# Weight sums of a seven-product scheme: high and low parts stored apart, low parts in two buffers, high parts' stores issued by ScalarE

## The chip, the cores and the metric

The kernel runs on one core of one Trainium2 chip. The metric is the device time in microseconds (us) of one launch; lower is better. The time before is 3198.1 us, the median of three runs (3197.61 to 3199.45).

## What is computed

Two branches read the same input x of 8192 tokens by 512 channels and are added to it: a state-space layer followed by a two-layer MLP with GELU (512 to 2048 to 512), and a gated feed-forward layer with block-wise FP4 rounding. The change lies in the preparation of the first MLP matrix w1.

```
xn = layernorm(x)
x  = x + attn_ref(xn, ...) + ffn_ref(xn, w_gate, w_up, w_down)
# inside attn_ref
x = x + ssm_scan(rmsnorm(x, scale1), A, B, C, D)
h = rmsnorm(x, scale2)
h = gelu(h @ w1 + b1) @ w2 + b2          # the MLP
return x + h
```

All of it is in float32. The kernel splits each factor of a matrix product into a high part (fp32r, a rounded copy) and a low part (the difference), and adds three products, high by high, high by low and low by high.

## The kernel before

The program first does the FP4 branch and the state-space layer (up to about 1750 us of the trace). The MLP follows in two manners. The first eight token tiles of 128 tokens, two blocks of four, are done plainly in a loop over steps n = 2 to 33: `mlp1(n)` is 12 matmuls into one bank (one slice of 128 hidden units), `gelu(n)` on ScalarE turns it into `gf`, `gelu_parts(n)` on VectorE makes its high and low parts, and `mlp2(n - 2)` is 12 more matmuls. Behind ScalarE's `gelu(n)` stands the wait for `mlp1(n)`, and `mlp1(n + 2)` waits for `gelu(n)`. In steps 2 to 13 ScalarE (`w_high`, line 1923) and VectorE (`w_low`, line 1527) also split the weight slice n + 2 that `mlp1(n + 2)` needs.

The other 56 tiles are done in seven pairs of blocks with a seven-product scheme (lines 1193 and 1215), which needs sums of quarters of w1. These sums are made beside the plain steps, in 16 rounds k. The helper `combine_steps` puts round k at step 3 + 4k//3, so three rounds fall on each four steps (3, 4, 5, 7, 8, 9, 11, ... 23). A round is, by engine:

- SyncE (SP), step of k less 1 or earlier: `combine_load` (line 751) loads a piece of w1 into `wt[:, k % 2]`, once `combine_low(k - 2)` is done.
- ScalarE (ACT): `combine_scale(k)` (line 1973), two instructions in `wt`.
- GpSimd (POOL): `combine_sums(k)` (lines 2201 to 2206), four sums of 128x128.
- ACT, one step later: `combine_high(k)` (line 1981) writes `wh`, of 128x1024. It waits for the sums and, through the count of `d_wa`, until both stores of round k - 1 have landed.
- POOL, the same step: `combine_low(k)` (line 2210), `wl = wt - wh`. It has no wait for a store of its own; that of `combine_high` covers it.
- SP, two steps after the round's own: `combine_store(k)` (line 759) stores `wh` and `wl`, 512 KB each, into `r_A` in device memory.

From step 18 on `ring_load` (line 768) reads `r_A` back into the ring of 14 buffers that the products read.

Every engine runs its instructions in program order, and the order within a step matters. On ACT a step is: `w_high(n + 2)`, `gelu(n)`, `combine_scale`, `combine_high`, then the work on a token tile (`tile_high`, line 1947, or `tile_square`, line 1929). On SP it is: `combine_store`, `combine_load`, then the loads and stores of a token tile. In steps 3 to 11 this is `quadrants` (lines 830 and 833: a store to `r_H`, a wait until it has landed, four loads back). In steps 15 to 25 it is, for each of the tiles 8 to 15 in turn, `store_sum` (716, `r_Q`), `store_normed` (720, `r_N`), `z_load` of the next tile (712, `zl`, which waits until the `r_Q` store has landed), and `pre_load` two tiles ahead (695 and 699, `xl` and two of `yl`). Two such tiles fall on three steps. POOL's `tile_z` (2189, 2192) adds into `zl`, and `store_sum` waits for it. At steps 24, 25, 29 and 31 SP also loads turned tiles (`quarters`, line 739), which VectorE's `conv_turn` (line 1600) transposes and ACT's `conv_high` (lines 2001 to 2010) splits; the first `conv_high` waits for all stores of the sums.

Of the kernel before, what the change touches and what calls it, by code (L numbers as in the profile page):

```python
# [5 lines left out]
ALU = mybir.AluOpType  # L6
ACT = mybir.ActivationFunctionType
F32 = mybir.dt.float32
F32R = mybir.dt.float32r
# [3 lines left out]
P = 128  # L13
TOK = 8192
NT = TOK // P
# [30 lines left out]
STEPS = ((A11, B11, 4), (S2, T2, 5), (S3, T3, 6), (A12, B21, 4), (S1, T1, 7), (A22, T4, 6), (S4, B22, 7))  # L46
OPENS = (0, 1, 2, 4)
WSC0, WSUM0, WAH0, WAL0, HT0 = 4 * NST, 4 * NST, 3, 4, 11
RING_0, OQ_0, ZQ_0, WT_0, Q_0, WA_0, QO_0 = 32, 16, 8 * NT, 16, 16, 16, 16
QUADS = ((0, 1), (2, 3), (4, 0), (1, 2))  # L50
TURNED = ((4, 0), (1, 2), (3, 4), (0, 1))
SECOND = [(0, f) for f in range(14)] + [(1, 0), (1, 1), (0, 14), (0, 15)] + [(1, f) for f in range(2, 16)]
# [139 lines left out]
def combine_steps(n):  # L192

    return [k for k in range(16) if 3 + 4 * k // 3 == n]
# [14 lines left out]
def build(nc, x, A, B, C, Dv, sc1, sc2, w1, b1, w2, b2, wg, wu, wd, cst, out):  # L209
# [12 lines left out]
    r_A = nc.dram_tensor("r_A", [8, 8, P, 512], F32, kind="Internal").ap()  # L222
    r_s = nc.dram_tensor("r_s", [D * NST], F32, kind="Internal").ap()

    with ExitStack() as ctx:
        def sbt(c, name, shape, dt=F32):
            return c.enter_context(nc.sbuf_tensor(name, shape, dt))

        def sem(name):
            return ctx.enter_context(nc.semaphore(name))  # L230

        def sems(name, n):
            return [sem(f"{name}{i}") for i in range(n)]
# [65 lines left out]
        mctx = ExitStack()  # L299
# [28 lines left out]
        with ExitStack() as later:  # L328
            u2 = sbt(later, "u2", [P, D])
            u3 = sbt(later, "u3", [P, D])  # L330
            G2x = sbt(later, "G2x", [P, 2, D], F32R)
        zx1 = sbt(mctx, "zx1", [P, 4, D])
        st = sbt(mctx, "st", [P, D])
        s1 = sbt(mctx, "s1", [P, D])
        with ExitStack() as later:
# [3 lines left out]
            HC = sbt(later, "HC", [P, 5, 2, 2, D], F32R)  # L339
        wt = sbt(mctx, "wt", [P, 2, 8, P])  # L340
        wh = sbt(mctx, "wh", [P, 8, P], F32R)
        wl = sbt(mctx, "wl", [P, 8, P], F32R)
        assert nc.sbuf_base == base_ssm
        hT0 = [sbt(mctx, f"hT0{h}", [P, KD, D], F32R) for h in range(2)]
        zx0 = sbt(mctx, "zx0", [P, 4, D])
# [40 lines left out]
        s_wsc, s_wsum, s_wah, s_wal, s_ht = s_kC, s_kK, s_ka, s_kR, s_kd  # L386
# [4 lines left out]
        d_cs, d_kin, d_xin, d_px = sem("d_cs"), sems("d_kin", 6), sems("d_xin", 4), sems("d_px", 4)  # L391
        d_rs, d_a128, d_rW, d_rK = sem("d_rs"), sem("d_a128"), sems("d_rW", 2), sem("d_rK")
# [5 lines left out]
        d_xl, d_yl, d_zl, d_oo = sems("d_xl", 2), sems("d_yl", 2), sem("d_zl"), sems("d_oo", 8)  # L398
        d_ho, d_hi = sems("d_ho", 2), sems("d_hi", 2)
        d_ring, d_oq, d_zq, d_wt, d_q, d_wa, d_qo = d_wl[0:14], d_oo[0:4], d_px, d_kin[0:2], d_kin[2:4], d_kin[4], d_kin[5]  # L400

        def slot(t):
            return 0 if t < 4 else t % 2
# [82 lines left out]
        def combined(m, h):  # L486

            if m < 5:
                return HC[:, m, h]
            return WH[:, 4 * (m - 5) + 2 * h:4 * (m - 5) + 2 * h + 2, 0:D]  # L490

        def ring(q):
            return Wp[q % 14][1][:, 0]
# [37 lines left out]
        def sync_program(e):  # L531
# [118 lines left out]
            def z_out(t):  # L650
                e.wait_ge(s_z, t + 1)
                e.dma_start(r_Z[t], xin[:, 2 + t % 2]).then_inc(d_zo[t % 2], 16)
# [90 lines left out]
            def combine_load(k):  # L743
                if k >= 16:
                    return
                u, kt = k // 2, k % 2
                if k == 0:
                    e.wait_ge(s_dn, NW)
                if k >= 2:
                    e.wait_ge(s_wal, WAL0 + k - 1)  # L750
                e.dma_start(wt[:, k % 2, 0:4].rearrange("p (a f) c -> p a (f c)", a=2),
                            bass.AP(w1.tensor, kt * P * 2048 + 256 * u, [[2048, P], [2 * P * 2048, 2], [1, 256]])
                            ).then_inc(d_wt[k % 2], 16)

            def combine_store(k):
                u, kt = k // 2, k % 2
                for h in range(2):
                    e.wait_ge((s_wah, s_wal)[h], (WAH0, WAL0)[h] + k + 1)
                    e.dma_start(bass.AP(r_A.tensor, u * 8 * P * 512 + 256 * h + P * kt, [[512, P], [P * 512, 8], [1, P]]),
                                (wh, wl)[h][:].bitcast(F32)).then_inc(d_wa, 16)  # L760

            def ring_load(q):
                if q >= 56 * PAIRS:
                    return
                if q < 14:
                    e.wait_ge(s_w1, 17 + q)
                    e.wait_ge(d_wa, WA_0 + 32 * 4)
                e.dma_start(ring(q).bitcast(F32), r_A[q // 7 % 8, STEPS[q % 7][0]]).then_inc(d_ring[q % 14], 16)  # L768

            def residual_in(c, i):  # L770
# [165 lines left out]
            for n in range(2, 16 * NB1 + 2):  # L936
                if n == 2:
                    z_out(NT - 2)
                    z_out(NT - 1)
                for k in combine_steps(n - 2):  # L940
                    combine_store(k)
                for k in combine_steps(n - 1):
                    combine_load(k + 2)
                if (n - 2) % 16 == 15:
                    for j in range(4):
                        t = 4 * ((n - 2) // 16) + j
                        e.wait_ge(s_o, t + 1)
                        e.dma_start(ot[t], zx[(n - 2) // 16 % 2][:, j]).then_inc(d_oo[t % 8], 16)
                for t, part in mlp_steps(n):
                    prepare(t, part)  # L950
                for o, part in early_steps(n):
                    if part == 1:
                        store_sum(o)
                        store_normed(o)
                        z_load(o + 1)
                        if o < OLD + 6:
                            pre_load(o + 2)
                        else:
                            quarters(0, o - OLD - 6)
                if 18 <= n < 32:  # L960
                    ring_load(n - 18)
                if n in (29, 31):
                    quarters(0, (n - 25) // 2)
# [298 lines left out]
        def vector_program(e):  # L1262
# [328 lines left out]
            def conv_turn(c, i):  # L1591

                e.wait_ge(d_q[i % 2], Q_0 + 128 * (2 * c + i // 2 + 1))
                if i == 0 and c:
                    e.wait_ge(s_hch, 20 * c)
                    e.wait_ge(s_hcp, 8 * c)
                for j in range(2):
                    if i or j:
                        e.wait_ge(s_ht, HT0 + 8 * c + 2 * i + j)
                    e.transpose(place5[TURNED[i][j]][:], place5[QUADS[i][j]][:]).then_inc(s_ht, 1)  # L1600
# [167 lines left out]
        def scalar_program(e):  # L1768
# [206 lines left out]
            def combine_high(k):  # L1975
                e.wait_ge(s_wsum, WSUM0 + 4 * (k + 1))
                if k:
                    e.wait_ge(d_wa, WA_0 + 32 * k)
                else:
                    e.wait_ge(s_dn, NW)  # L1980
                e.activation(wh[:], wt[:, k % 2], ACT.Copy).then_inc(s_wah, 1)

            def conv_high(c, i, x):
                HA, HB = [place5[TURNED[i][j]] for j in range(2)]
                ba, bb = sum_banks(c, i)
                at = slice(i * P, (i + 1) * P)
                if c == 0 and i == 0 and x == 0:
                    e.wait_ge(s_w1, 24)
                    e.wait_ge(d_wa, WA_0 + 32 * 16)
                    for j in range(4):  # L1990
                        e.wait_ge(d_oo[j], 16)
                elif c and i == 0 and x == 0:
                    e.wait_ge(s_p, 56 * c)
                if x < 2:
                    e.wait_ge(s_ht, HT0 + 8 * c + 2 * i + 2)
                elif x == 2:
                    e.wait_ge(s_ts, 16 * c + 4 * i + 3)
                else:
                    e.wait_ge(s_ts, 16 * c + 4 * i + 4)
                if x == 0:  # L2000
                    e.activation(HC[:, B11:B21 + 1, 0, :, at], HA[:].rearrange("p (m k t) -> p m k t", m=2, k=2),
                                 ACT.Copy).then_inc(s_hch, 1)
                elif x == 1:
                    e.activation(combined(B22, 0)[:, :, at], HB[:, 256:512].rearrange("p (k t) -> p k t", k=2),
                                 ACT.Copy).then_inc(s_hch, 1)
                elif x == 2:
                    e.activation(HC[:, T1:T3 + 1, 0, :, at], ba[:].rearrange("p (m k t) -> p m k t", m=2, k=2),
                                 ACT.Copy).then_inc(s_hch, 1)
                else:
                    e.activation(combined((T2, T4)[x - 3], 0)[:, :, at],  # L2010
                                 bb[:, 256 * (x - 3):256 * (x - 2)].rearrange("p (k t) -> p k t", k=2),
                                 ACT.Copy).then_inc(s_hch, 1)
# [72 lines left out]
        def gpsimd_program(e):  # L2085
# [121 lines left out]

            def combine_low(k):
                e.wait_ge(s_wah, WAH0 + k + 1)
                e.tensor_tensor(wl[:], wt[:, k % 2], wh[:].bitcast(F32), ALU.subtract).then_inc(s_wal, 1)  # L2210

            def conv_low(c, i):
                HA, HB = [place5[TURNED[i][j]] for j in range(2)]
# [120 lines left out]
```

## Time and profile before

| | us |
|---|---|
| median of three runs | 3198.1 |
| the profiled execution, its own time | 3199.24 |
| span of its trace | 3197.4 |
| TensorE matmul busy | 3016.1 |
| VectorE busy | 2179.4 |
| GpSimd busy | 1599.9 |
| ScalarE busy | 1156.7 |

PE is TensorE's matmul side, DVE is VectorE, ACT is ScalarE, POOL is GpSimd, SPq is SyncE's queue of DMA issues. PEclk is the granted TensorE clock as a share of full speed. "A <- B" in a list of waits reads: the engine and line A stood idle until B. All DMAs of the program are issued by SP.

### The profile page before, as it was taken

Reading aid. Unit: us, or ns where it says so; the run is one execution under the profiler, and the core shown is the slowest. Engines: PE = TensorE matmul, PEld = TensorE weight load, DVE = VectorE, ACT = ScalarE, POOL = GpSimd, SP = SyncE. Lnnn points to the kernel's source line nnn. Section 1 sums busy time; section 2 is a strip of 40 time slices with the busy share of each in tenths; the row PEclk is TensorE's granted clock in tenths of the full one; section 3 lists DMA queues with packets and bytes.
Section 4 is the critical chain, followed back from the end, with each engine's and each line's share of the span. In section 5 each row is a group of like instructions: output and inputs, shape, how many; then the busy total and the mean of one; then the engine's idle time right before and its main releaser. Section 6 shows DMA issues by size and latency. Waiting matters only on the chain. (4 is left out here: it accounts for less than half of the span.)

```text
span 3197.4 us, 44061 instructions
## 1 busy us (share of the span) xinstructions
PE 3016.1 (94%) x14525; PEld 2427.6 (76%) x14525; DVE 2179.4 (68%) x4455; ACT 1156.7 (36%) x1930; POOL 1599.9 (50%) x1457
## 2 busy tenths in 40 slices
PE   5899999999999999999999666899999999999999
PEld 3677878888877777777777445687888787878787
DVE  8799898887777767677776555656565656565622
ACT  5345665544544433434323322322222222222220
POOL 7556666655555555455553444345353545353413
PEclk9999999999999999999999878999999999999999
DMA  4133334357766666666545457777867686868541
GB/s 125 48 90 101 108 107 117 103 149 184 187 166 170 172 159 159 176 154 160 150 92 135 125 149 195 197 207 172 211 172 199 180 209 163 222 160 217 141 132 50
DMA packets 975794, 488.77 MB, mean 153 GB/s; under 512 B 689232, under 2 KB 817488, under 8 KB 973008
## 3 DMA queue, kind: packets, MB, share of 16 engines
q1 hardware_dynamic: 975568, 485.96, 58.4%
q8 instruction: 118, 1.93, 0.3%
q14 instruction: 108, 0.88, 0.1%
HBM read 346.84 MB, written 138.97 MB: 152 GB/s over the span
## 5 line engine op out<-in xcount | busy, mean ns | idle before, releaser
L1019 PE MATMUL bank<-XT,Wg 128*128 128x512 f32 (+1 forms) x2148 | 525.3, 394 | 6.3 <-DVE Wd L1371 6.3
L1019 PE MATMUL bank<-XT,Wu 128*128 128x512 f32 (+1 forms) x2148 | 516.4, 390 | 15.3 <-DVE sg L1304 14.8
L1041 PE MATMUL bank<-Wd,HT 128*128 128x512 f32 x2112 | 515.8, 393 | 6.5 <-POOL HT L2115 5.2
L1019 PEld LDWEIGHTS bank<-XT,Wu 128*128 128x128 f32 x2148 | 402.3, 190 | 105.2 <-issue 24.1
L2107 POOL TENSOR_TENSOR qa<-qb,qs 128x512 f32<-128x512 f32 (+2 forms) x277 | 308.1, 1113 | 344.2 <-DVE qb L1364 341.8
L1041 PEld LDWEIGHTS bank<-Wd,HT 128*128 128x128 f32 x2112 | 392.5, 188 | 105.7 <-issue 15.4
L1019 PEld LDWEIGHTS bank<-XT,Wg 128*128 128x128 f32 x2148 | 399.8, 191 | 94.7 <-DVE Wd L1371 8.3
L1215 PE MATMUL bank<-Wp,G 128*128 128x512 f32 x1800 | 456.9, 391 | 5.3 <-POOL G L2226 5.2
L1193 PE MATMUL bank<-HC,Wp 128*128 128x512 f32 x1680 | 423.5, 391 | 2.8 <-POOL WH L2219 2.8
L1215 PEld LDWEIGHTS bank<-Wp,G 128*128 128x128 f32 x1800 | 336.9, 188 | 79.7 <-POOL G L2226 10.5
L1193 PEld LDWEIGHTS bank<-HC,Wp 128*128 128x128 f32 x1680 | 316.8, 189 | 68.7 <-POOL WH L2219 3.2
L2115 POOL TENSOR_TENSOR HT<-qb,HT 128x512 fp32r<-128x512 f32 (+1 forms) x179 | 229.5, 1282 | 242.1 <-ACT HT L1804 241.9
L2101 POOL TENSOR_TENSOR qa<-qa,qs 128x512 f32<-128x512 f32 (+1 forms) x243 | 262.6, 1080 | 109.3 <-DVE qs L1344 109.3
L1804 ACT ACTIVATE HT<-qb 128x512 fp32r<-128x512 f32 (+1 forms) x179 | 112.2, 627 | 412.8 <-DVE qb L1318 412.7
L2226 POOL TENSOR_TENSOR G<-gf,G 128x512 fp32r<-128x512 f32 x75 | 103.3, 1378 | 301.6 <-DVE G L1648 301.6
L1215 PE MATMUL bank<-Wp,G2x 128*128 128x512 f32 x888 | 229.2, 391 | 3.3 <-POOL G2x L2226 3.3
L1356 DVE SCALAR_TENSOR_TENSOR qa<-qb,qa 128x512 f32<-128x512 f32 (+2 forms) x149 | 120.7, 810 | 141.0 <-ACT qb L1776 140.8
L1215 PEld LDWEIGHTS bank<-Wp,G2x 128*128 128x128 f32 x888 | 166.2, 188 | 39.9 <-POOL G2x L2226 5.8
L1142 PE MATMUL bank<-hT,Wp 128*128 128x512 f32 x384 | 115.5, 460 | 81.3 <-ACT gf L1964 38.2
L1811 ACT ACTIVATE sg<-bank 128x512 f32<-128x512 f32 (+1 forms) x179 | 105.5, 589 | 205.3 <-PE bank L1019 201.9
L1193 PE MATMUL bank<-WH,Wp 128*128 128x512 f32 x672 | 171.3, 391 | 5.0 <-DVE GX L1674 2.6
L1339 DVE TENSOR_REDUCE qs<-qa 128x32 f32<-128x512 f32 (+1 forms) x243 | 165.2, 680 | 8.3
(199 smaller groups left out, 4435.6 us busy)
## 6 DMA issues: line engine op xcount, KB each, us to landing
Wp<-r_A SPq DMA_DIRECT2D x392, 256.0 KB, 3.4
px<-in_L_attn_x_dram SPq DMA_DIRECT2D x128, 256.0 KB, 3.3
xin<-in_L_attn_x_dram SPq DMA_DIRECT2D x128, 256.0 KB, 3.4
sT<-r_K SPq DMA_DIRECT2D x128, 256.0 KB, 4.2
r_Z<-xin SPq DMA_DIRECT2D x64, 256.0 KB, 2.4
r_U<-ub SPq DMA_DIRECT2D x16, 1024.0 KB, 6.7
sU<-r_U SPq DMA_DIRECT2D x32, 512.0 KB, 5.1
r_Y<-sY SPq DMA_DIRECT2D x16, 1024.0 KB, 5.5
```

Source lines behind the costliest of these rows:

```text
L1019: ins = e.matmul(bk[:, 0:n], W[wh][:, k, :], inputs(xh, w, k), start=(k == 0 and p_ == 0), stop=(k == KD - 1 and p_ == 2))
L1041: ins = e.matmul(DNB[t % 4][:], HT[hh][:, w % 2, a * P:(a + 1) * P], Wd[wh][:, f, :], start=(w == first(n) and p_ == 0), stop=(w == last(n ...
L1142: ins = e.matmul(bk[:], Wp[f][wh][:, 0, k * P:(k + 1) * P], hT[xh][b % 2][:, k, :], start=(k == 0 and p_ == 0), stop=(k == KD - 1 and p_ = ...
L1193: ins = e.matmul(bank[bk][:], ring(q)[:, 256 * wh_ + P * kt:256 * wh_ + P * kt + P], combined(b, xh)[:, kt], start=(k in OPENS and kt == 0 ...
L1215: ins = e.matmul(bank[4 * half + j][:], (second_high(q), second_low(q))[gh][:, j * P:(j + 1) * P], Wp[f][wh_][:, 1, :], start=(f == 0 and ...
L1339: e.tensor_reduce(s_, blk(job_in(m)), AX, ALU.max, apply_absolute_value=True).then_inc(s_mx, 1)
L1356: e.scalar_tensor_tensor(Aa, Bb, FLOOR, Aa, ALU.max, ALU.add).then_inc(s_t, 1)
L1804: e.activation(HT[0][:, w % 2, 0:n], qb[:, m % 2, 0:n], ACT.Copy).then_inc(s_hh, 1)
L1811: e.activation(sg[:, 0:n], GB[:, 0:n], ACT.Silu).then_inc(s_sg, 1)
L2101: e.tensor_tensor(blk(qa[:, m % 4, 0:n]), blk(job_in(m)), bc(qs[:, m % 4, 1, 0:n // 16], n // 16), ALU.mult).then_inc(s_pa, 1)
L2107: e.tensor_tensor(blk(qa[:, m % 4, 0:n]), blk(qb[:, m % 2, 0:n]), bc(qs[:, m % 4, 0, 0:n // 16], n // 16), ALU.mult).then_inc(s_ph, 1)
L2115: e.tensor_tensor(lo, qb[:, m % 2, 0:n], hi.bitcast(F32), ALU.subtract).then_inc(s_hl, 1)
```

## The change

Three things change. `combine_store` is split: ACT's `combine_high` issues the store of `wh` itself, right behind the instruction that writes it, and SP's `store_sums_low` keeps the store of the low part, at the same place in SP's order. The low part gets two buffers used in turn (the second lies where `st` and `s1` lie later). And the waits are divided: `combine_high(k)` waits for the landing of the previous high part's store alone and for `combine_low(k - 1)` (which still reads `wh`), while `combine_low(k)` waits for the landing of the low part's store of round k - 2. The waits of the users of `r_A` and of the place of the second buffer (`conv_turn`) are adapted.

```diff
-            def combine_store(k):
-                u, kt = k // 2, k % 2
-                for h in range(2):
-                    e.wait_ge((s_wah, s_wal)[h], (WAH0, WAL0)[h] + k + 1)
-                    e.dma_start(bass.AP(r_A.tensor, u * 8 * P * 512 + 256 * h + P * kt, [[512, P], [P * 512, 8], [1, P]]),
-                                (wh, wl)[h][:].bitcast(F32)).then_inc(d_wa, 16)
+            def store_sums_low(k):
+                e.wait_ge(s_wal, WAL0 + k + 1)
+                e.dma_start(sums_place(k, 1), wl[k % 2][:].bitcast(F32)).then_inc(d_wb[k % 2], 16)
...
                 for k in combine_steps(n - 2):
-                    combine_store(k)
+                    store_sums_low(k)
...
+                elif i == 0:
+                    e.wait_ge(d_wb[1], WB_0 + 16 * 8)
...
             def combine_high(k):
                 e.wait_ge(s_wsum, WSUM0 + 4 * (k + 1))
                 if k:
-                    e.wait_ge(d_wa, WA_0 + 32 * k)
+                    e.wait_ge(d_wa, WA_0 + 16 * k)
+                    e.wait_ge(s_wal, WAL0 + k)
                 else:
                     e.wait_ge(s_dn, NW)
                 e.activation(wh[:], wt[:, k % 2], ACT.Copy).then_inc(s_wah, 1)
+                e.wait_ge(s_wah, WAH0 + k + 1)
+                e.dma_start(sums_place(k, 0), wh[:].bitcast(F32)).then_inc(d_wa, 16)
...
             def combine_low(k):
                 e.wait_ge(s_wah, WAH0 + k + 1)
-                e.tensor_tensor(wl[:], wt[:, k % 2], wh[:].bitcast(F32), ALU.subtract).then_inc(s_wal, 1)
+                if k >= 2:
+                    e.wait_ge(d_wb[k % 2], WB_0 + 16 * (k // 2))
+                e.tensor_tensor(wl[k % 2][:], wt[:, k % 2], wh[:].bitcast(F32), ALU.subtract).then_inc(s_wal, 1)
```

## Rows read from the trace of the kernel before

**Rows 1.** The page: span, and slices of 79.9 us (busy tenths, granted clock).
```profile
span 3197.4 us, 44061 instructions
...
PE   5899999999999999999999666899999999999999
...
PEclk9999999999999999999999878999999999999999
```

**Rows 2.** Stretches: length, busy us of the five engines, granted clock, DMA share, GB/s.
```profile
1758.40:1879.90 121.50, 72.42 (x250) 55.31 (x249) 63.85 (x107) 39.05 (x79) 56.88 (x55) 0.80 0.50 129
1879.90:2000.90 121.00, 83.87 (x307) 65.31 (x305) 60.36 (x144) 25.36 (x51) 51.67 (x50) 0.82 0.73 188
2000.90:2029.50 28.60, 22.35 (x96) 17.88 (x96) 19.41 (x41) 10.47 (x24) 8.39 (x9) 1.00 0.60 130
...
2050.00:2140.00 90.00, 90.00 (x398) 74.59 (x397) 50.85 (x126) 25.11 (x42) 35.44 (x26) 1.00 0.84 216
```

**Rows 3.** Waits from 1758 to 2001 us: total us, times, longest.
```profile
ACT wh L1981 <- DMA r_A<-wl: 115.5, 14, 16.2
...
PE bank L1142 <- ACT gf L1964: 35.9, 6, 10.6
PE bank L1142 <- DVE Wp L1527: 27.4, 7, 8.1
...
PE bank L1142 <- DVE hT L1563: 15.7, 1, 15.7
...
ACT HC L2001 <- DMA r_A<-wl: 10.9, 1, 10.9
```

**Rows 4.** ACT in order of time, rounds 0 to 2: start, us, idle before.
```profile
1764.07 1.06 ACT L1981 ACTIVATE wh<-wt 128x1024 fp32r<-128x1024 f32 x1 [4.17 <-POOL wt L2206]
...
1777.15 1.06 ACT L1981 ACTIVATE wh<-wt 128x1024 fp32r<-128x1024 f32 x1 [4.17 <-DMA r_A<-wl]
...
1792.54 1.06 ACT L1981 ACTIVATE wh<-wt 128x1024 fp32r<-128x1024 f32 x1 [12.72 <-DMA r_A<-wl]
```

**Rows 5.** SP's DMA issues in order of time, the same rounds.
```profile
1780.65 0.37 SPq L751 DMA_DIRECT2D wt<-in_L_attn_w_dram  x1
...
1784.46 2.60 SPq L833 DMA_DIRECT2D xl<-r_H  x4
1787.10 0.63 SPq L759 DMA_DIRECT2D r_A<-wh  x1
1787.77 0.58 SPq L759 DMA_DIRECT2D r_A<-wl  x1
```

**Rows 6.** Groups by line, 1758 to 2001 us: busy us, mean ns, idle before.
```profile
L2210 POOL TENSOR_TENSOR wl<-wt,wh 128x1024 fp32r<-128x1024 f32 x16 | 38.2, 2389 | 83.6 <-ACT wh L1981 83.6
...
L1973 ACT ACTIVATE wt<-wt,vec 128x256 f32<-128x256 f32 x30 | 13.6, 501 | 26.1 <-DMA wt<-in_L_attn_w_dram 26.1
...
L2202 POOL TENSOR_TENSOR wt<-wt 128x128 f32<-128x128 f32 x16 | 10.5, 657 | 0.0
```

**Rows 7.** DMA issues of 1760 to 1880 us: count, KB, median us to landing.
```profile
r_A<-wh SPq DMA_DIRECT2D x8, 512.0 KB, 4.1
r_A<-wl SPq DMA_DIRECT2D x8, 512.0 KB, 5.1
wt<-in_L_attn_w_dram SPq DMA_DIRECT2D x9, 256.0 KB, 3.0
```

**Rows 8.** SP's DMA issues in order of time, one tile's circuit at step 22.
```profile
1963.00 0.32 SPq L712 DMA_DIRECT2D zl<-r_Z  x1
...
1969.41 2.10 SPq L716 DMA_DIRECT2D r_Q<-zl  x1
...
1974.67 0.32 SPq L712 DMA_DIRECT2D zl<-r_Z  x1
```

**Rows 9.** The DMA issues on r_A: ns of the issue, least, median, most.
```profile
L768 SPq DMA_DIRECT2D Wp<-r_A x392: 319/327/3025, 1935.1 to 3114.7; - x196
L759 SPq DMA_DIRECT2D r_A<-wh x16: 432/529/2757, 1771.5 to 1994.5; - x16
```

More of the change, by code:

```diff
@@ L48 @@
 WSC0, WSUM0, WAH0, WAL0, HT0 = 4 * NST, 4 * NST, 3, 4, 11
-RING_0, OQ_0, ZQ_0, WT_0, Q_0, WA_0, QO_0 = 32, 16, 8 * NT, 16, 16, 16, 16
+RING_0, OQ_0, ZQ_0, WT_0, Q_0, WA_0, WB_0, QO_0 = 32, 16, 8 * NT, 16, 16, 16, 16, 16
 QUADS = ((0, 1), (2, 3), (4, 0), (1, 2))
@@ L332, in build @@
         zx1 = sbt(mctx, "zx1", [P, 4, D])
+        with ExitStack() as later:
+            wl1 = sbt(later, "wl1", [P, 8, P], F32R)
         st = sbt(mctx, "st", [P, D])
@@ L341, in build @@
         wh = sbt(mctx, "wh", [P, 8, P], F32R)
-        wl = sbt(mctx, "wl", [P, 8, P], F32R)
+        wl = [sbt(mctx, "wl0", [P, 8, P], F32R), wl1]
         assert nc.sbuf_base == base_ssm
@@ L400, in build @@
         d_ring, d_oq, d_zq, d_wt, d_q, d_wa, d_qo = d_wl[0:14], d_oo[0:4], d_px, d_kin[0:2], d_kin[2:4], d_kin[4], d_kin[5]
+        d_wb = [d_cs, d_rs]
         def slot(t):
@@ L490, in combined, with sums_place @@
             return WH[:, 4 * (m - 5) + 2 * h:4 * (m - 5) + 2 * h + 2, 0:D]
+        def sums_place(k, h):
+            return bass.AP(r_A.tensor, k // 2 * 8 * P * 512 + 256 * h + P * (k % 2), [[512, P], [P * 512, 8], [1, P]])
         def ring(q):
@@ L766, in ring_load @@
                     e.wait_ge(s_w1, 17 + q)
-                    e.wait_ge(d_wa, WA_0 + 32 * 4)
+                    e.wait_ge(d_wa, WA_0 + 16 * 4)
+                    for i in range(2):
+                        e.wait_ge(d_wb[i], WB_0 + 16 * 2)
                 e.dma_start(ring(q).bitcast(F32), r_A[q // 7 % 8, STEPS[q % 7][0]]).then_inc(d_ring[q % 14], 16)
@@ L1988, in conv_high @@
                     e.wait_ge(s_w1, 24)
-                    e.wait_ge(d_wa, WA_0 + 32 * 16)
+                    e.wait_ge(d_wa, WA_0 + 16 * 16)
+                    for j in range(2):
+                        e.wait_ge(d_wb[j], WB_0 + 16 * 8)
                     for j in range(4):
```

## The prediction

> **What bounds the kernel now.** I began with the page's slices: TensorE is at nine tenths or more nearly everywhere, except in three slices around 1840 to 2080 us, where it is at six tenths and the granted clock is down as well [rows 1]. That is the only large hole, and the rounds k lie in it. So the second view is the table of stretches. I cut at the start of gelu(4) (1758.4), the start of gelu(15) (1879.9) and the issue of the last `zl` load of the plain steps (2000.9). The first two stretches are 242.5 us long, hold 557 matmuls and have 156.3 us of busy TensorE [rows 2]. What would these matmuls take unhindered? The stretch from 2050 to 2140 us holds 398 in 90.0 us, so 0.226 us each, 2.7 us for twelve and 5.4 us for a step n [rows 2]. 557 of them are 126 us. The hole is therefore 116 us: 86 us of idle TensorE, and 30 us in which it is busy but slow, at a granted clock of 0.80 and 0.82 against 1.00. I count the slow part as a result of the idleness, for both stretches before which TensorE did not stand still are at 1.00.
>
> Third, the waits: who is late? TensorE waits for `gelu` (35.9 us), for the low parts of weight slices (27.4) and for `hT` (15.7). All three are made from something ACT does in its order, and ACT itself stood 115.5 us, 14 times, before `wh`, with the stores of the previous round as the last to arrive [rows 3]. That the 115.5 and the 116 agree is partly chance: ACT has slack of its own.
>
> Fourth, one round in order of time, to see what that wait is made of. Round 1's `wh` starts at 1777.15, round 2's at 1792.54: 15.4 us apart, 12.7 of it waiting [rows 4]. Behind `wh` (1.06) comes POOL's `wl` (2.39 on the mean [rows 6]); then SP issues the next `wt` load at 1780.65, stores to `r_H`, waits for that to land, issues four loads (2.60), and only at 1787.10 and 1787.77 the two stores [rows 5]. The second lands about 5 us later, which frees ACT. So 6.4 us of the 15.4 are SP doing things that have nothing to do with the round, ahead of stores that ACT waits for. ACT's `gelu` and `w_high` of the next step stand behind that wait.
>
> **The change part by part.** *Removed: the wait of `wh` for the low part's store and for SP's position.* What is late next? `wh` of round k now needs its own predecessor's store: 1.06 us of `wh`, a short handshake, an issue (0.53 us, the median on SP [rows 9]) and a landing of 4.1 us from issue [rows 7], together about 6 us between two `wh` (6.2 with the handshake). The sums of round k + 2 need another circuit: `wh`, `wl`, SP's load of `wt` (3.0 us from issue to landing [rows 7]), two scalings (2 x 0.50 [rows 6]), four sums (the four lines are alike, one is 0.66 us [rows 6], about 2.4 us in all).
>
> I then walked one group of three rounds, four steps, through all engines' orders with these durations. From `wh` of the first round: POOL has the sums of the next round ahead of `wl` (2.5 + 2.4, with the 0.2 between), 0.4 for the issue and 3.0 to land, 0.9 for the scaling: 9.4 us to the second `wh`. Then 6.2 to the third, for the store. Then 3.5 (`wh` and `wl`), 2.3 because SP is still at its quadrant loads of the tile, 3.2 for the load, 0.9 for the scaling: 9.9. The group takes 25.5 us. TensorE's own four steps are 21.8, so this chain and not TensorE is the bound, narrowly. The first stretch is eleven steps, 2.75 groups: 70 us, and 5.7 us to the first `wh` at 1764.1 [rows 4], which nothing changes: 76 us against 121.5, a gain of 45.5. Bounds: the DMA engines were busy 0.50 of 121.5, 61 us, so 68 at nine tenths (gain 54); with 5 us more for each group's three waits under a fuller queue, 90 (gain 31).
>
> *The second stretch* has the token tiles 8 to 15. Here SP's own list becomes the bound: from one `zl` load (1963.00) over POOL's additions, the `r_Q` store (1969.41) and its landing to the next `zl` load (1974.67) it is 11.7 us, in a place where SP waited for no sum [rows 8]. Eight such circuits are 94 us, against 8 x 8.2 us that TensorE would allow (two tiles in three steps). Against that stands the transfer itself. The stretch moves 121.0 us x 188 GB/s, 22.7 MB [rows 2]. At the 216 GB/s that the steady stretch behind shows, at a share of 0.84, that is 105 us; at this stretch's own 188/0.73 and nine tenths busy (232 GB/s), 98 us. I take 100 us, a gain of 21, between 27 (94 us) and 9 (112 us, the circuit stretched by a fifth).
>
> A rule of the Trainium skill speaks against counting on a second queue. "DMA: Bandwidth & Descriptors", section "Issuing engines are not separate DMA queues", says that transfers run on the same 16 DMA engines whoever issues them, and that issuing from more engines saves only the issue time. By that rule the 105 us bound on the second stretch stands although ACT now issues half of the stores; without it the stretch would go by the tile circuit of 94 us, and the whole would come to a gain of 68 and not 62. No row of before can show it, since SP issues everything there.
>
> *Added: 16 issues on ACT.* None is in the trace on ACT. The nearest rows are SP's own: 0.43 at least, 0.53 in the middle, 2.76 at most [rows 9]. ACT is busy 39 and 25 us in the two stretches [rows 2], so most of it fits. `gelu` of the next step stands behind it. I take 0.53, 8.5 us in all, half of it on the path: 4 us. Bounds: 0, and 16 x 2.76 = 44 us, all on the path. A gain from the issue as such is excluded, since ACT did nothing of the kind before. The same 16 issues leave SP; this is in the second stretch's circuit, and worth no more than 8.5 us there, hidden behind the transfers.
>
> *Added waits.* `wl` waits for the low store of round k - 2: that store has at least a step (5.4 us) and mostly two, against a landing of 5.1 [rows 7], so nothing; if SP falls a step behind, POOL's `tile_z` queues behind this wait and the tile circuit grows, which is in the 112 us above. `wh` waits for `wl` of the round before: done in time, as the walk shows. `conv_turn` waits for the last low store. ACT stood 10.9 us for that store already [rows 3], so it is exposed, and two transposes and their sums now come behind it, some 3 us; but the stretch from 2000.9 to 2029.5 goes by SP's further `quarters` loads and TensorE is at 22.4 of 28.6 us [rows 2]. I take 0, bounds 0 and 3. After 2029.5 nothing changes.
>
> **The sum.** 45.5 + 21 - 4 = 62 us (62.5). Against the profiled execution's own 3199.24 (span 3197.4 [rows 1] and 1.8 around it) that gives 3137; it stands 1.1 above the median of 3198.1, and against the median it is 3136.
>
> **The rivals.** *A, the issue on ACT is dear.* Every store is issued while other descriptors queue; if it takes ACT the 2.76 us of SP's worst case, 16 x (2.76 - 0.53) = 36 us are added ahead of `gelu`: gain 62 - 36 = 26, 3172. For it: SP's long issues fall together with busy transfers, and transfers get denser. Against: the median is 0.53.
>
> *B, TensorE becomes the bound.* If the walk is too strict and the waits fold into slack, the gain goes up to what the transfers allow: 54 + 27, less nothing: 81, 3117. The full 116 us (3082) is excluded, since the transfers' 61 + 88 = 149 us of busy time would not fit into 126.
>
> *C, slower.* ACT's issue waits until the queue has room for all descriptors of a 512 KB store. From 62/16 + 0.53 = 4.4 us for each issue the gain is gone; at 6 us it would be 16 x 5.5 - 66.5, 21 us slower: 3219. The longest issue seen is 3.03 [rows 9], so it needs what no row shows.
>
> *D, the wait only moves.* If SP is so late that `wl` waits for the store of round k - 2 as long as `wh` waits now, `wt` loads, which wait for `wl`, keep the old pace: 3198. Against: SP's own list, without waits for the sums, is shorter than the stretch.
>
> **How the numbers follow.** The forecast, with its own bounds (31 + 9 - 4 = 36 to 81 us of gain), has 0.72; A 0.12; B beyond it 0.07; D 0.04; C 0.03; the small rest of 0.02 is a gain between D and A. The range goes from B's 3117, a little under it, to A's 3172: 3114 to 3173. Faster by over 0.2% (6.4 us, about what a measurement of this kernel can tell from no change): 0.93. Same: D and a part of the rest, 0.04. Slower: 0.03.
>
> **What would show it.** In the profile after, the wait of `wh` for a store should fall from 115.5 to under 35 us, and its releaser should be the store of `wh`. The stretch from gelu(4) to gelu(15) should be near 76 us, that from there to the last `zl` load near 100, with a DMA share of 0.85 or more. TensorE's slow-clock excess should shrink with its idleness. ACT's waits for `wt` loads should be what remains in the first stretch, SP's `r_Q` and tile loads in the second. An ACT issue of more than 2 us would point to A; long waits of `wl` for `r_A<-wl` to D. The prediction is wrong if the second stretch stays near 121 us, or if the first goes by TensorE.

## The result and the profile after

The changed kernel takes 3141.0 us, the median of four runs (3139.3 to 3143.0), beside 3197.9 for the kernel before in the same four rounds. The ratio is 0.9825, with a 95% interval of 0.9808 to 0.9842: 57 us less, where 62 were forecast. The span of its profiled execution is 3140.6 us against 3197.4.

The page of the changed kernel first: the span, then the rows that answer to [rows 1], slices of 78.5 us, and the share of the DMA engines.

```profile
span 3140.6 us, 44091 instructions
...
PE   5899999999999999999999877999999999999999
...
PEclk9999999999999999999999998999999999999999
DMA  4133334357766666666633788777777676768541
```

The hole is shallower and shorter, and the granted clock falls in one slice only. The same three stretches as in [rows 2], cut at the start of gelu(4), of gelu(15), at the last `zl` load of the plain steps and at the first matmul of the seven-product scheme, and a steady stretch behind (length, busy us of the five engines, granted clock, DMA share, GB/s):

```profile
1757.70:1841.40 83.70, 63.17 (x252) 48.65 (x251) 67.50 (x107) 39.21 (x79) 56.07 (x55) 0.95 0.74 192
1841.40:1942.30 100.90, 77.93 (x300) 61.79 (x299) 67.02 (x139) 25.34 (x49) 50.98 (x50) 0.88 0.86 221
1942.30:1971.20 28.90, 23.86 (x103) 18.78 (x101) 21.78 (x47) 11.35 (x25) 8.39 (x9) 1.00 0.58 129
1992.00:2082.00 90.00, 90.00 (x399) 74.53 (x398) 50.84 (x126) 25.58 (x44) 35.35 (x25) 1.00 0.82 212
```

The first stretch went from 121.5 to 83.7 us, the second from 121.0 to 100.9, the third from 28.6 to 28.9. The first two give 57.9 us. Behind the first matmul of the scheme the rest is 1169.3 us against 1167.9. The two stretches now hold 552 matmuls. At 0.226 us each they are 124.8 us, so 59.8 us are lost where 116 were: 43.5 of idleness and 16.3 of slow clock (141.1 busy less 124.8). Matmuls at the lower clock went down with the idleness, 30 to 16 us, as the prediction assumed.

Who waited, from 1758 to 1945 us (total us, times, longest), to be read beside [rows 3]:

```profile
ACT yl L1936 <- DVE xl L1541: 45.0, 9, 10.8
POOL zl L2201 <- DMA zl<-r_Z: 30.9, 6, 8.4
...
ACT wt L1980 <- DMA wt<-in_L_attn_w_dram: 24.1, 7, 9.0
...
PE bank L1147 <- ACT gf L1971: 12.7, 5, 6.0
...
ACT wh L1989 <- POOL wt L2218: 12.4, 3, 7.7
...
PE bank L1147 <- DVE Wp L1532: 11.7, 5, 3.9
...
ACT wh L1989 <- DMA r_A<-wh: 8.3, 3, 3.4
...
POOL wl L2224 <- DMA r_A<-wl: 4.3, 2, 2.2
DVE st L1607 <- DMA r_A<-wl: 4.0, 1, 4.0
...
PE bank L1147 <- DVE hT L1568: 4.0, 1, 4.0
...
ACT wh L1989 <- POOL wl L2224: 3.4, 2, 1.8
```

ACT's 115.5 us before `wh` are 24.1 us now, a third of it for a store. The list is headed by the token tile: ACT before its squares (`yl` is the place they are written to) waits for VectorE's sum `xl`, and POOL for SP's load of `zl`. VectorE stood idle for no load of `xl` or `yl` in this window. It came late by its own list, and in the second stretch by 12.2 us of waiting for POOL's `zl`.

The same rounds in order of time as in [rows 4], now with ACT's own issue between them:

```profile
1772.14 1.04 ACT L1989 ACTIVATE wh<-wt 128x1024 fp32r<-128x1024 f32 x1
1773.21 0.37 ACTq L1991 DMA_DIRECT2D r_A<-wh  x1
1773.62 1.15 ACT L1930 ACTIVATE Wp<-Wr 128x512 fp32r<-128x512 f32 x2 [0.44 <-ACT wh L1989]
1774.68 0.67 ACT L1971 ACTIVATE gf<-bank,vec 128x512 f32<-128x512 f32 x1
1777.13 1.06 ACT L1989 ACTIVATE wh<-wt 128x1024 fp32r<-128x1024 f32 x1 [1.77 <-POOL wl L2224]
1778.21 0.39 ACTq L1991 DMA_DIRECT2D r_A<-wh  x1
1783.46 1.14 ACT L1954 ACTIVATE hT<-bank,vec 128x128 fp32r<-128x128 f32 x4 [5.27 <-DVE bank L1565]
```

Rounds 1 and 2 are 5.0 us apart, where [rows 4] had 15.4. Then ACT stands 5.27 us for a transposition on VectorE, which the prediction had not in its walk. In that time VectorE was not idle (its rows first, then POOL's):

```profile
1778.24 3.48 DVE L1532 TENSOR_TENSOR Wp<-Wr,Wp 128x512 fp32r<-128x512 f32 x2
...
1782.70 0.72 DVE L1565 STREAM_TRANSPOSE bank<-xl 128x512 f32<-128x512 f32 x1
...
1785.67 1.28 DVE L1532 TENSOR_TENSOR Wp<-Wr,Wp 128x512 fp32r<-128x512 f32 x2
```

```profile
1778.26 2.91 POOL L2224 TENSOR_TENSOR wl<-wt,wh 128x1024 fp32r<-128x1024 f32 x1 [1.25 <-ACT wh L1989]
```

The same pair of `w_low` took 3.48 us beside POOL's `wl` and 1.28 us while POOL was idle, and the transposition stands behind it.

### The profile page after: what moved, and what is told of

Same layout as the page of the kernel before. It is cut to its first block and busy times, and to the rows that moved or that the text cites. A ratio compares the mean times of both kernels' runs of the same rounds, so it can differ in the third digit from the quotient of the medians.

```text
span 3140.6 us, 44091 instructions
## 1 busy us (share of the span) xinstructions
PE 3003.5 (96%) x14525; PEld 2415.9 (77%) x14525; DVE 2190.5 (70%) x4455; ACT 1158.1 (37%) x1930; POOL 1602.3 (51%) x1457
## 5 line engine op out<-in xcount | busy, mean ns | idle before, releaser
L1024 PEld LDWEIGHTS bank<-XT,Wu 128*128 128x128 f32 x2148 | 401.3, 190 | 106.6 <-issue 25.7
L1046 PEld LDWEIGHTS bank<-Wd,HT 128*128 128x128 f32 x2112 | 391.6, 188 | 106.0 <-issue 15.4
L1323 DVE STREAM_TRANSPOSE qb<-qa 128x512 f32<-128x512 f32 (+1 forms) x179 | 124.9, 698 | 55.5 <-POOL qa L2119 55.5
```

Source lines behind the costliest of these rows:

```text
L1024: ins = e.matmul(bk[:, 0:n], W[wh][:, k, :], inputs(xh, w, k), start=(k == 0 and p_ == 0), stop=(k == KD - 1 and p_ == 2))
L1046: ins = e.matmul(DNB[t % 4][:], HT[hh][:, w % 2, a * P:(a + 1) * P], Wd[wh][:, f, :], start=(w == first(n) and p_ == 0), stop=(w == last(n ...
L1323: e.transpose(qb[:, m % 2, 0:n], qa[:, m % 4, 0:n]).then_inc(s_t2, 1)
```

## The experiments

Each is compared with the kernel before on the same chip in the same rounds. The kernel before had 3201.0 us beside "high store back on SP", "one low buffer", "stores a step earlier" and "low stores on ACT too", and 3197 to 3198 beside the others, so gains are told from the ratios, times 3198 us: the changed kernel's 0.9825 is 56 us. Intervals of the ratio are about 0.0015 (5 us) to each side, so two kernels that differ by 5 us or so are told apart by the stretches of their traces at best, and by one trace each. "First" and "second" in the table are the first two stretches, cut in each trace at the same instructions (83.8 and 100.8 us for the changed kernel are the 83.7 and 100.9 of above, cut to the hundredth).

| kernel | us | ratio to before, interval | first | second |
|---|---|---|---|---|
| before | 3197.9 | | 121.5 | 121.0 |
| changed | 3141.0 | 0.9825 (0.9808 to 0.9842) | 83.8 | 100.8 |
| high store back on SP | 3189.1 | 0.9962 (0.9948 to 0.9976) | 112.8 | 116.4 |
| one low buffer | 3172.1 | 0.9910 (0.9892 to 0.9927) | 98.6 | 114.4 |
| before, stores a step earlier | 3165.5 | 0.9893 (0.9877 to 0.9909) | 98.9 | 111.3 |
| high store early, on SP | 3146.3 | 0.9841 (0.9826 to 0.9856) | 86.6 | 102.4 |
| low stores on ACT too | 3143.5 | 0.9826 (0.9810 to 0.9841) | 86.5 | 99.4 |
| extra tiny DMA | 3143.1 | 0.9831 (0.9817 to 0.9846) | 84.3 | 101.2 |
| extra 512 KB a round | 3150.5 | 0.9857 (0.9841 to 0.9874) | 86.0 | 107.1 |
| wt loads on POOL | 3141.2 | 0.9827 (0.9812 to 0.9841) | 85.1 | 98.6 |
| tile loads ahead of zl | 3159.2 | 0.9879 (0.9864 to 0.9893) | 83.8 | 119.0 |
| plain yl loads | 3136.3 | 0.9804 (0.9789 to 0.9819) | 83.8 | 95.7 |
| transposition a step later | 3147.5 | 0.9841 (0.9825 to 0.9857) | 86.3 | 102.5 |
| two places for zl | 3139.7 | 0.9814 (0.9801 to 0.9827) | 83.6 | 97.6 |

**Which part of the change brings the gain?** My theory was SP's position: other work stood in SP's list ahead of stores that ACT waited for. First, the high store goes back to SP, and everything else of the change stays:

```diff
             def store_sums_low(k):
+                e.wait_ge(s_wah, WAH0 + k + 1)
+                e.dma_start(sums_place(k, 0), wh[:].bitcast(F32)).then_inc(d_wa, 16)
                 e.wait_ge(s_wal, WAL0 + k + 1)
...
                 e.activation(wh[:], wt[:, k % 2], ACT.Copy).then_inc(s_wah, 1)
-                e.wait_ge(s_wah, WAH0 + k + 1)
-                e.dma_start(sums_place(k, 0), wh[:].bitcast(F32)).then_inc(d_wa, 16)
```

> The changed kernel with one part undone: SP issues the high store again, at its old place two steps behind the round; the two low buffers and the divided waits stay. My theory is that SP's position ahead of the store was what cost (6.4 of 15.4 us in the round read from the trace of before), so most of the gain of 57 us should go again: the wait of wh for a store comes back to 50 to 90 us, and the time is 3165 to 3185. The rival, that the gain came from the low store leaving the wait of wh, expects 3141 to 3150.

Measured 3189.1 us. By the ratio only 12 us of the gain are left, less than I had expected. The high store's wait is back. The waits of that kernel from 1755 to 2000 us ("issue" means that the profile shows nothing that ended the wait):

```profile
ACT wh L1991 <- DMA r_A<-wh: 51.6, 5, 14.2
...
ACT wh L1991 <- issue: 28.1, 5, 7.9
```

Divided waits and two low buffers bring 12 of the 56 us as long as the high store is issued two steps late.

Second, the two low buffers become one:

```diff
-        wl = [sbt(mctx, "wl0", [P, 8, P], F32R), wl1]
+        wl0 = sbt(mctx, "wl0", [P, 8, P], F32R)
+        wl = [wl0, wl0]
...
-                if k >= 2:
-                    e.wait_ge(d_wb[k % 2], WB_0 + 16 * (k // 2))
+                if k:
+                    e.wait_ge(d_wb[(k - 1) % 2], WB_0 + 16 * ((k + 1) // 2))
```

> The changed kernel with a single low buffer: wl of a round waits until the low store of the round before has landed, which SP issues at its old place; ACT still issues the high stores. Theory of SP's position: the wait moves from ACT's wh to POOL's wl, the next wh waits for wl, so nearly all is lost again, 3180 to 3200. Rival, that the issue by ACT alone brings the gain: 3141 to 3155.

Measured 3172.1 us, between both expectations: by the ratio 29 us of gain, so the second buffer is worth 27 of the 56 us. The wait moved as the theory said. The waits of that kernel from 1755 to 2000 us:

```profile
ACT wt L1981 <- DMA wt<-in_L_attn_w_dram: 60.8, 10, 10.6
POOL wl L2225 <- DMA r_A<-wl: 58.5, 11, 10.0
...
ACT wh L1990 <- POOL wl L2225: 26.6, 5, 9.6
```

POOL's `wl` waits 58.5 us, so the next `wt` load is late, and ACT waits 60.8 us for that.

Third, the kernel before with SP's stores moved up by one step, ahead of the tile's work:

```diff
-                for k in combine_steps(n - 2):
-                    combine_store(k)
                 for k in combine_steps(n - 1):
                     combine_load(k + 2)
+                    combine_store(k)
```

> The kernel before with one edit: SP issues both stores one step earlier, right behind the load of the next wt and ahead of the work on the token tile. One buffer, joint wait, no DMA issued by ACT. If SP's position is the cause, this alone takes the 6.4 us of other work out of each round's circuit and brings 30 to 57 us: 3141 to 3168. If a second buffer or a second issuing engine is needed, it stays at 3185 to 3198.

Measured 3165.5 us. Moving two issues in SP's list, with one buffer and the joint wait, brings 34 of the 56 us. ACT's wait for `r_A<-wl` is a half of the 115.5 us (waits from 1755 to 2000 us):

```profile
ACT wh L1980 <- DMA r_A<-wl: 55.9, 12, 9.6
```

Six of the first eight rounds are 9.6 to 10.2 us apart there. `wh` (1.06), `wl` (2.4), the issues ahead of the landing (about 1) and the low store's landing (5.2, the median) make 9.7. So what is left of the wait is in the main the landing of the low store, which comes after `wl`; the divided wait and the second buffer take that away.

Fourth, the changed kernel with the high store on SP, but early:

```diff
                 for k in combine_steps(n - 1):
+                    e.wait_ge(s_wah, WAH0 + k + 1)
+                    e.dma_start(sums_place(k, 0), wh[:].bitcast(F32)).then_inc(d_wa, 16)
                     combine_load(k + 2)
```

> The changed kernel, but the high store is issued by SP, one step earlier than before and ahead of the wt load and of the work on the token tile; low stores, two buffers and divided waits as in the changed kernel. If only SP's position cost and the issuing engine does not matter, this gives the whole gain: 3139 to 3150. If an issue by ACT is needed because SP gets to this place late anyhow (its list is full in the second stretch), 3155 to 3175.

Measured 3146.3 us, by the ratio 51 of the 56 us; its interval overlaps that of the changed kernel. So nearly all of the gain hangs on the moment of the issue and not on the engine that issues. The rule in the prediction says the same (the Trainium skill, "DMA: Bandwidth & Descriptors", section "Issuing engines are not separate DMA queues"). The traces agree with it but for 4.4 us: the two stretches are 86.6 and 102.4 us against 83.8 and 100.8. The use of ACT is that it reaches the place at once, whatever SP's list does. With SP the wait for the store is 16.8 us, against 8.3 (waits of ACT from 1757 to 1990 us):

```profile
ACT wh L1991 <- DMA r_A<-wh: 16.8, 3, 8.1
```

**Is the issue on ACT dear (rival A)?** One more DMA of 2 KB behind each high store, which nobody reads:

```diff
                 e.dma_start(sums_place(k, 0), wh[:].bitcast(F32)).then_inc(d_wa, 16)
+                e.dma_start(r_B[k, 0:1, 0], b2r[0:1]).then_inc(d_x, 16)
```

> The changed kernel with one more DMA in each of the 16 rounds, issued by ACT right behind the high store: 2 KB from b2r into a spare tensor that nobody reads or waits for. It prices the issue on ACT. By the prediction an issue costs ACT about half a microsecond, half of it on the path: 0 to 5 us more than the changed kernel, 3141 to 3146. Rival A (an issue holds ACT for 2 us and more) expects 3165 or more.

Measured 3143.1 us, 2 us more for 16 issues, within the spread of the runs. Rival A, which needs 36 us for 16 issues, is out.

**What bounds the second stretch?** Three candidates: transfers, SP's list, the circuit over `zl`. For the transfers, two DMAs of 256 KB more behind each high store, in pieces of 512 bytes:

```diff
+                e.dma_start(r_B[k, :, 0].rearrange("p (a b) -> p a b", b=P), b2r[:].rearrange("p (a b) -> p a b", b=P)).then_inc(d_x, 16)
+                e.dma_start(r_B[k, :, 1].rearrange("p (a b) -> p a b", b=P), b2r[:].rearrange("p (a b) -> p a b", b=P)).then_inc(d_x, 16)
```

> The changed kernel with two more DMAs of 256 KB in each round, issued by ACT behind the high store, in chunks of 512 bytes into a spare tensor that nobody reads: 8.4 MB more, about 4 MB in each of the two stretches. It tests whether transfers bound them. If the second stretch (DMA share 0.86 after) goes by the transfers, its 22.4 MB become 26 and it gets about 15 us longer; the first stretch (share 0.74) has room for a part: in all 15 to 30 us more, 3156 to 3171. If SP's order and the circuits of waits bound both, at most 8 us more: under 3149.

Measured 3150.5 us, 9.5 more than the changed kernel, between the two expectations. The first two stretches of that kernel:

```profile
1757.30:1843.30 86.00, 65.78 (x248) 51.51 (x247) 62.06 (x107) 39.21 (x79) 56.97 (x55) 0.88 0.91 244
1843.30:1950.40 107.10, 83.18 (x309) 65.48 (x308) 59.92 (x139) 25.20 (x49) 51.29 (x50) 0.86 0.90 240
```

The second stretch carries 25.7 MB (107.1 x 240) instead of 22.3 and takes 6.3 us longer, not the 15 of a stretch that goes by the transfers. The first carries 21.0 MB instead of 16.1 and takes 2 us longer. 240 GB/s at a share of 0.90 also shows that the 216 GB/s, from which my bound of 105 us came, was no ceiling.

For SP's list, the low stores go to ACT too (all but the last):

```diff
                 e.activation(wh[:], wt[:, k % 2], ACT.Copy).then_inc(s_wah, 1)
+                if k:
+                    j = k - 1
+                    e.dma_start(sums_place(j, 1), wl[j % 2][:].bitcast(F32)).then_inc(d_wb[j % 2], 16)
```

> The changed kernel with the low stores issued by ACT too (each behind the next wh; the last one stays on SP), so SP has 15 fewer issues of 0.43 to 2.4 us. If SP's own list bounds the second stretch, it becomes 5 to 15 us shorter, 3128 to 3136. If the transfers bound it (DMA share 0.86 there), nothing changes: 3138 to 3143.

Measured 3143.5 us: no change. And the `wt` loads go to POOL, so that SP does not wait for `wl`:

```diff
-                for k in combine_steps(n - 1):
-                    combine_load(k + 2)
...
                 e.tensor_tensor(wl[k % 2][:], wt[:, k % 2], wh[:].bitcast(F32), ALU.subtract).then_inc(s_wal, 1)
+                if k + 2 < 16:
+                    e.wait_ge(s_wal, WAL0 + k + 1)
+                    if k:
+                        e.wait_ge(d_wp, 16 * k)
+                    e.dma_start(wt[:, k % 2, 0:4].rearrange("p (a f) c -> p a (f c)", a=2),
...
+                                ).then_inc(d_wp, 16)
```

> The changed kernel with the loads of wt for rounds 2 to 15 issued by POOL, right behind the wl that frees the buffer, instead of by SP, which waited 36.2 us for that wl with the tile's loads and stores queued behind. If SP's waiting in its list is what is left, ACT's waits for xl (45.0 us) and for wt (24.1) shrink and the time is 3120 to 3136. If the transfers bound the second stretch, it is 3136 to 3143. If the issue on POOL is dear, it is slower than 3145.

Measured 3141.2 us: no change either, although SP's 36.2 us of waits before that load are gone. The second stretch is 98.6 us there, the first 85.1. Neither of the two things that the rounds put on SP bounds by itself what is left.

For the circuit, SP's order within a tile is turned:

```diff
                         store_normed(o)
-                        z_load(o + 1)
                         if o < OLD + 6:
                             pre_load(o + 2)
-                        else:
+                        z_load(o + 1)
+                        if o >= OLD + 6:
                             quarters(0, o - OLD - 6)
```

> The changed kernel with SP's order turned in steps 15 to 22: the xl and yl loads of the tile two ahead are issued before the zl load of the next tile, not after it. In the second stretch ACT waits 30 us for xl and POOL 31 us for zl. If the loads of xl and yl are what is late, the stretch of 101 us gets 3 to 8 us shorter (3133 to 3138). If the circuit over zl and r_Q is the bound, as the prediction has it (11.7 us a tile), each turn gets 3 us longer: 15 us or more slower, 3155 and over.

Measured 3159.2 us, 18 more. The whole of it is in the second stretch, 119.0 against 100.8, and the first is 83.8 in both. The waits in a part of that stretch, 1842 to 1943 us:

```profile
POOL zl L2201 <- DMA zl<-r_Z: 50.3, 6, 11.9
DVE xl L1553 <- POOL zl L2204: 34.1, 5, 10.7
```

Six tiles (9 to 14 turned) times the 3 us of the issues put ahead of `zl` are 18 us. The six circuits grew unevenly, by 0.5 to 6.3 us each, but by 19 in sum. So the circuit from `zl` load to `zl` load is on the path, as the prediction had it.

Then the same tiles' `yl` in one DMA with rows of 2 KB. This leaves out the right gathering of the scan's result, so it is for timing only:

```diff
+                if OLD <= o < OLD + 8:
+                    e.dma_start(yl[k][:], bass.AP(r_Y.tensor, t * P * D, [[D, P], [1, D]])).then_inc(d_yl[o % 2], 32)
+                    return
                 for i in range(2):
```

> The changed kernel, but the eight tiles 8 to 15 load their yl, 256 KB, in one DMA with rows of 2 KB instead of two DMAs in pieces of 64 bytes; the values are from other places of r_Y, so this leaves out the right gathering of the scan's result for these tiles. Same bytes, 8 issues and about 16 us of issue time on SP less, and far fewer packets. If the second stretch goes by packets and SP's issue time in the tile's work, it gets 10 us or more shorter: 3120 to 3131. If it goes by the latencies of zl and r_Q alone: 3138 to 3143.

Measured 3136.3 us, 5 less than the changed kernel, between the two expectations; the intervals of the ratios overlap, but the 5 us are all in the second stretch, which is 95.7. Its share of the DMA engines fell to 0.75 at 233 GB/s (changed: 0.86 at 221). The small pieces fill the DMA engines and SP's list, and cost some 5 us between them; which of the two costs was not tried.

Last, a second place for `zl` for three of the tiles, so that five loads need not wait for the landing of `r_Q`:

```diff
+        def z_place(o):
+            return zx0[:, 0] if o in (11, 13, 15) else zl[:]
...
-                if o > OLD:
+                if o == 11:
+                    e.wait_ge(d_oo[0], 16)
+                if o > OLD and not 11 <= o <= 16:
                     e.wait_ge(d_qo, QO_0 + 16 * (o - OLD))
-                e.dma_start(zl[:], r_Z[t]).then_inc(d_zl, 16)
+                e.dma_start(z_place(o), r_Z[t]).then_inc(d_zl, 16)
```

> The changed kernel with a second place for zl (the first tile of zx0, free from step 17 to 25) for tiles 11, 13 and 15, so that five of the zl loads no longer wait until the r_Q store of the tile before has landed (16.5 us of SP's waits in the second stretch). If the circuit over zl and r_Q bounds the second stretch, up to 5 times 3 us come off it, less what the fuller transfers and SP's tile loads take back: 5 to 12 us, 3129 to 3136. If the transfers or SP's issue time are just as late, it stays at 3138 to 3142.

Measured 3139.7 us, and its interval overlaps that of the changed kernel: not a version that can be called faster. The second stretch is 97.6 us, 3 less, but the third is 32.0 and not 28.9. SP's waits in that kernel from 1842 to 1940 us say where the time went:

```profile
SPq L704 <- DMA r_N<-xl: 10.7, 6, 3.1
...
SPq L722 <- DMA r_Q<-zl: 3.5, 2, 2.4
```

The 16.5 us for `r_Q` are 3.5, and 10.7 us for `r_N` stand in their place: the next load in the list waits for the other store's landing.

**What was left out of the first stretch?** It took 83.8 us where the walk gave 76. ACT's new wait was the one for VectorE's transposition, 12.8 us in all. So that part was moved by a step:

```diff
-    at = [(2, 3, 6), (4, 5, 8), (8, 9, 12), (10, 11, 14)]
+    at = [(2, 3, 7), (4, 5, 9), (8, 9, 13), (10, 11, 15)]
```

> The changed kernel with the last part of each of the tiles 4 to 7 (transposition on VectorE, the split on ACT and VectorE, the tile loads two ahead on SP) one step later. In the first stretch (83.8 us, 76 predicted) ACT waited 12.8 us for that transposition, which stands behind w_low in VectorE's order. If this is the term that the prediction left out, the first stretch gets 3 to 8 us shorter, 3133 to 3138; if the late tile loads cost as much, it stays within 3 us of 3141.

Measured 3147.5 us, 6 more (the intervals of the ratios overlap), and the first stretch is 86.3. The move made new waits. From 1842 to 1943 us:

```profile
PE bank L1147 <- DVE hT L1568: 14.0, 1, 14.0
```

TensorE waited 14 us for `hT` of the second block, finished a step later. In the first stretch ACT's wait for the transposition fell from 12.8 to 7.2 us and that for `wt` rose from 4.1 to 11.2. So the transposition is one late arrival among several, not the term by itself.

## Why the prediction was right, step by step

*What bounds, and why.* The hole of 116 us was the right place, all 57 us came out of it. That SP's unrelated work ahead of the stores is the cause was read from one round [rows 4, 5]; the early stores in the kernel before (34 us gained) and the late high store in the changed one (44 us lost by the ratios) show it.

*The first stretch: mis-sized by 8 us.* 76 us were forecast, 83.8 measured, within the bounds of 68 and 90. Three rounds were to take 25.5 us; from `wh` 0 to 3 to 6 they took 26.9 and 27.9 (1763.33, 1790.26, 1818.13), and the last three steps 23.3 instead of 19.1. Of the three intervals, forecast at 9.4, 6.2 and 9.9 us, the first two came out well (8.8 and 5.0, then 9.8 and 5.7); the third was too long both times, 13.1 and 12.4. The walk had no time of VectorE's in it. ACT stands before the tile's work in the same step, and by the trace of after that is 12.8 us for VectorE's transposition and 14.9 for its `xl` in the first stretch. TensorE stood 20.5 us there, 18.2 of them for VectorE's results (11.7 for `w_low`, 4.0 for `hT`, 2.5 for the low part of `gf`). VectorE was busy for 67.5 of the 83.7 us and waited for no load. Its work took longer than it could have: in each group of the same line and shape, I took the shortest instruction as the time undisturbed, and the sum over the stretch is 25 us above that, nearly all of it in instructions that ran beside one of POOL's. The plainest case works on one column (least, median and most in ns, 1757 to 1842 us):

```profile
L1289 DVE TENSOR_TENSOR rs<-rs x9: 159/385/2320, 1773.8 to 1818.8; 128x1 f32<-128x1 f32 x9
```

No run takes this away, so it is not shown that the stretch would then reach 76. In the first group SP was late as well: the `wt` load went out at 1784.44 and landed 4.5 us later, where the walk has about 1783 and 3.2. Taking the low stores or the `wt` loads from SP made the stretch no shorter (86.5 and 85.1 us), nor did a later transposition (86.3). More bytes, 4.9 MB, cost it 2 us.

*The second stretch: right in size, in part by luck.* 100 us forecast, 100.8 measured. That the tile circuit is on the path holds: one more delay in it for six tiles cost 18 us. But it does not run as eight circuits of 11.7 us, one place in the trace of before. In the trace of after the first `zl` load comes 6.6 us into the stretch, and seven circuits of 9.4 to 19.2 us follow, 94.2 in all. Two are shorter than the 11.7. The two longest are 19.2, in which SP stands 7.4 us for `wl` ahead of a `wt` load, and this one of 18.1, in which SP issues almost without a pause from 1862.24 to 1876.71:

```profile
1861.67 0.32 SPq L718 DMA_DIRECT2D zl<-r_Z  x1
...
1868.54 4.44 SPq L953 DMA_DIRECT2D out_dram<-zx  x4
...
1879.73 0.32 SPq L718 DMA_DIRECT2D zl<-r_Z  x1
```

That the start and the uneven circuits add up to the forecast is luck. The transfers were given too much weight: their bound of 105 us would have made the extra 3.4 MB cost about 15 us, and they cost 6.3. The small pieces of `yl` are worth 5 us of the 100.8.

*The issue on ACT: 4 us forecast.* It was not measured by itself; 16 further, small ones cost about 2 us, within the spread. Each issue of the high store took 0.37 us instead of 0.53, with no long one (0.394 at most). The row of after, least, median and most in ns:

```profile
L1991 ACTq DMA_DIRECT2D r_A<-wh x16: 366/367/394, 1764.4 to 1921.8; - x16
```

*The added waits.* `wl` waits 4.3 us for a low store, nothing that shows; `conv_turn` waits 4.0 us and the third stretch is 0.3 us longer, so 0 was right.

*What was to be seen.* ACT's wait before `wh` is 24.1 us, under the 35 named; but the store of `wh` makes only 8.3 of it, the sums 12.4, and `wl` 3.4. The share of the DMA engines in the second stretch is 0.86, as named. The waits for `wt` loads, expected in the first stretch, are in the second: 20.0 of 24.1 us.

*The rivals.* A, a dear issue on ACT, is out by the tiny DMA; C, a slower kernel, by issues of 0.37 us; D, the wait that only moves, by the 4.3 us before `wl`. B, TensorE as the bound, was not reached: TensorE stood idle for 43.5 us of the two stretches. Nor did the transfers keep the first stretch from B, for it carried 4.9 MB more in 2 us more.

## What to carry to other kernels

When an engine waits for a DMA that another engine issues, look at what stands ahead of the issue in that engine's list; here moving two issues up by one step was worth 34 us with no other change. A buffer's release is only as early as the latest store that shares its semaphore, so a divided wait and a second buffer pay once the issue is early, and little before (12 us here). When the largest wait is gone, expect the next list to bound, on the same queue or on another engine: a walk needs the durations of every engine, VectorE here too, and from places where its neighbours run. One place is little to size a circuit from: 11.7 us stood here for circuits of 9.4 to 19.2.

## What the runs showed that I had not expected

An issue of the same shape took ACT 0.366 to 0.394 us in all 16 cases, while SP's low stores of the same size in the same trace went from 0.43 to 2.37 us. The four longest (1.21 to 2.37 us) stand right behind SP's two `yl` issues, as here:

```profile
1862.62 2.84 SPq L705 DMA_DIRECT2D yl<-r_Y  x2
1865.50 2.37 SPq L763 DMA_DIRECT2D r_A<-wl  x1
```

ACT's issues fell into the same stretches, with the DMA engines as full. That makes it likely that an issue gets long by what the same engine issued just before. The run with the extra 512 KB a round bears it out on ACT: its high store, the first of three issues, kept to 0.377 to 0.441 us, and the third, of 256 KB, went up to 2.17:

```profile
L1996 ACTq DMA_DIRECT2D r_B<-b2r x16: 455/1158/2172, 1765.1 to 1930.0; - x16
```

It was not tried by itself. Nor was the other thing that was seen, that VectorE's instructions take their least time, within 12 ns, where POOL is idle, and up to nearly fifteen times that beside one of POOL's (159 and 2320 ns for the same 128x1 instruction).
